# Lower mixture layer: one PE loop of five laps with the last tile's logits inside it, residual and store in halves

## The reference

```python
x = x + xattn(layernorm(x), ctx)        # 32 sequences of 64 rows, 512 wide; keys from ctx (1601 rows)
x = x + attn(layernorm(x))              # causal self-attention, 16 heads
x = x + ffn(layernorm(x))               # the mixture:

def kmoe(x_flat, W_router, A, B, scale, bias, ...):      # 64 experts, top 2
    logits = x_flat @ W_router.T
    vals, idx = jax.lax.top_k(logits, 2)
    probs = softmax(vals)
    xs = x_flat.reshape(-1, d_in1, d_in2)
    Y = einsum('nkoi,nij,nkpj->nkop', A[idx], xs, B[idx])
    return einsum('nkop,nk->nop', Y, probs).reshape(-1, d_out1 * d_out2) * scale + bias

h = gelu(kmoe(x_flat, up...))           # upper layer: rows of 32x32 to 64x64
y = kmoe(h, down...)                    # lower layer: rows of 64x64 back to 32x32
```

## Time and profile before

| | us |
|---|---|
| median of 3 runs | 1514.75 |
| the three runs | 1506.93, 1514.75, 1524.37 |
| the profiled execution, its own time | 1523.18 |
| its span (first to last instruction) | 1521.4 |
| mean granted TensorE clock, share of full | 0.935 |
| PE busy in the span | 1350.5 (89%) |
| DVE busy | 823.1 (54%) |
| ACT busy | 438.3 (29%) |
| POOL busy | 208.2 (14%) |

### The profile page before, as it was taken

One profiled execution on the slowest core, in us unless ns is written; L12 is line 12 of the kernel. 1 busy time (PEld: TensorE's weight loads), 2 busy tenths in 40 slices (PEclk: granted clock), 3 DMA queues, 4 the chain that ended last, 5 costly groups with the idle time before them and its releaser, 6 DMA issues.

```text
span 1521.4 us, 70167 instructions
## 1 busy us (share of the span) xinstructions
PE 1350.5 (89%) x32072; PEld 932.3 (61%) x32072; DVE 823.1 (54%) x1519; ACT 438.3 (29%) x879; POOL 208.2 (14%) x361
## 2 busy tenths in 40 slices
PE   7896799999999999889999999967888988798896
PEld 4895444444544454356666666646777876687785
DVE  1224566666665665145566555633647465347656
ACT  0230121112211221111122222203636455336544
POOL 0000000000000000001111111102424424023212
PEclk9798899999999999999999999968999999959968
DMA  5476187867886789251100111130203012532202
GB/s 194 143 219 217 38 281 273 269 210 278 300 254 213 279 291 285 72 106 56 51 28 31 55 55 42 56 84 30 111 28 139 38 73 105 222 146 87 107 28 83
DMA packets 57228, 211.96 MB, mean 139 GB/s; under 512 B 11760, under 2 KB 28144, under 8 KB 42640
## 3 DMA queue, kind: packets, MB, share of 16 engines
q1 hardware_dynamic: 57104, 210.14, 40.5%
HBM read 172.37 MB, written 37.75 MB: 138 GB/s over the span
## 4 chain that ended last, share of the span: by engine, by line
PE 42%; DVE 6%; issue 5%; ACT 2%; POOL 2%; DMA 1%; SPq 0%; DVEq 0%; POOLq 0%; ACTq 0%
PE ps L895 8%; PE ps L1675 5%; PE ps L1629 4%; PE ps L886 4%; PE ps L996 4%; PE ps L1644 3%; PE ps L1661 2%; PE ps L1718 2%; PE ps L1600 2%; PE ps L916 2%; PE ps L1701 2%; PE ps L1591 1%; PE ps L906 1%; DMA arena<-h_n 1%; PE ps L938 1%
## 5 line engine op out<-in xcount | busy, mean ns | idle before, releaser
L476 DVE STREAM_TRANSPOSE arena<-arena 128x384 f32<-128x384 f32 (+1 forms) x512 | 275.6, 586 | 133.2 <-PE ps L563 132.7
L563 PE MATMUL ps<-arena 32*64 32x224 f32 (+3 forms) x8192 | 241.3, 348 | 30.3 <-issue 22.0
L563 PEld LDWEIGHTS ps<-arena 32*64 32x64 f32 x8192 | 160.6, 134 | 140.9 <-DVE arena L476 85.8
L587 PE MATMUL ps<-arena 128*64 128x512 f32 (+1 forms) x832 | 207.1, 609 | 0.6 <-issue 0.6
L895 PE MATMUL ps<-arena 128*128 128x256 f32 x512 | 116.3, 386 | 6.2 <-ACT arena L847 6.2
L1515 ACT COPY arena<-ps 128x512 f32<-128x512 f32 x128 | 75.1, 587 | 149.8 <-PE ps L1644 79.4
L895 PEld LDWEIGHTS ps<-arena 128*128 128x128 f32 x512 | 97.1, 192 | 21.7 <-ACT arena L847 7.2
L534 ACT ACTIVATE arena<-ps,arena 128x416 f32<-128x416 f32 (+2 forms) x80 | 41.1, 530 | 229.1 <-DVE arena L488 229.1
L587 PEld LDWEIGHTS ps<-arena 128*64 128x64 f32 (+1 forms) x832 | 49.3, 136 | 86.7 <-issue 86.7
L1675 PE MATMUL ps<-arena 64*64 64x32 f32 x4096 | 91.6, 245 | 10.6 <-DVE arena L1352 5.7
L1675 PEld LDWEIGHTS ps<-arena 64*64 64x64 f32 x4096 | 85.8, 164 | 16.0 <-issue 12.5
(11 more groups left out here) (135 smaller groups left out, 1879.0 us busy)
## 6 DMA issues: line engine op xcount, KB each, us to landing
arena<-ctx SPq DMA_DIRECT2D x32, 1792.0 KB
arena<-ctx SPq DMA_DIRECT2D x32, 1280.0 KB
arena<-q_n SPq DMA_DIRECT2D x64, 256.0 KB, 14.0
h_n<-arena SPq DMA_DIRECT2D x16, 1024.0 KB, 4.4
arena<-h_n SPq DMA_DIRECT2D x16, 1024.0 KB, 9.9
arena<-x SPq DMA_DIRECT2D x16, 512.0 KB, 4.6
x_n<-arena SPq DMA_DIRECT2D x16, 512.0 KB, 3.1
arena<-x_n SPq DMA_DIRECT2D x16, 512.0 KB, 3.9
```

The costliest lines, as they stand in the source:

```text
L476: vec.transpose(z[:, at % RING, :, 0:nt * 32].rearrange("p b (j t) -> p b j t", t=32), slots[slot_of(k)][:, :, 0:nt, db * 32:(db + 1) * 32 ...
L563: last = pe.matmul(ps[b * SEQ:(b + 1) * SEQ, tb, g * 224:g * 224 + w], qs[p % 2][r, db, b * SEQ:(b + 1) * SEQ], z[r, at % RING, b, 0:w], s ...
L587: last = pe.matmul(ps[b * SEQ:(b + 1) * SEQ, OB, :], probt[0:r, j, b * SEQ:(b + 1) * SEQ], slot[0:r, b, jj, :], start=j == 0, stop=j == TI ...
```

## The change

The PE loop over tiles becomes a loop over five laps. Lap 0 does the first loop iteration (steps 0 and 1) of tile 0 and then the last tile's logits and their fold. Lap k, from 1 to 4, does the other six iterations of tile k-1, its last two `second_dn`, and the gather of tile k if there is one. The first and last index of the inner loop come out of the lap's number by register arithmetic. PE's wait for the copied logits is gone. On DVE, `parts` and `logits` move from ahead of step 0 to behind `y_out(1)`. `residual` works on halves of 512 columns, behind `y_out` of steps 3, 5, 7 and 9, and SP stores each half by itself; the counts of `s_res` and `s_end` follow.

```diff
             def store_out(T):
                 for t in range(2):
-                    sp.wait_ge(s_res, 2 * T + t + 1)
-                    sp.dma_start(out_v[2 * T + t, :, :], x2b[:, t, :]).then_inc(s_end, 16)
-                sp.wait_ge(s_end, 32 * T + 32)
+                    for half in range(2):
+                        r = slice(half * D, (half + 1) * D)
+                        sp.wait_ge(s_res, 4 * T + 2 * t + half + 1)
+                        sp.dma_start(out_v[2 * T + t, :, r], x2b[:, t, r]).then_inc(s_end, 16)
+                sp.wait_ge(s_end, 64 * T + 64)
...
-            def residual(T, t):
+            def residual(T, t, half):
+                r = slice(half * D, (half + 1) * D)
                 vec.wait_ge(s_x2, 32 * T + 32)
                 vec.wait_ge(s_yt, 2 * T + t + 1)
-                vec.scalar_tensor_tensor(x2b[:, t, :], yt[:, t, :], scales[:, 1:2], x2b[:, t, :],
+                vec.scalar_tensor_tensor(x2b[:, t, r], yt[:, t, r], scales[:, 1:2], x2b[:, t, r],
                                          ALU.mult, ALU.add).then_inc(s_res, 1)
...
-                if T == 0:
-                    parts(T_N, 6)
-                    logits("dn", T_N - 1, 6)
                 for n in range(STEPS):
                     if n + 2 < STEPS:
                         stage_h(T, n + 2)
                     y_out(T, n)
-                    if T and n in (3, 5):
-                        residual(T - 1, n // 5)
+                    if T and n in (3, 5, 7, 9):
+                        residual(T - 1, *divmod((n - 3) // 2, 2))
                     if T == 0:
+                        if n == 1:
+                            parts(T_N, 6)
+                            logits("dn", T_N - 1, 6)
...
-            def steps_dn(T):
-                with pe.Fori(T * 8, T * 8 + 7) as i:
+            def steps_dn(lap):
+                past = [(lap + T_N - k) // T_N for k in range(1, T_N + 1)]
+                whole = past[2] + past[3]
+                with pe.Fori(past[0] + past[1] * 7 + whole * 8, past[0] * 6 + (past[1] + whole) * 8 + 1) as i:
                     second_dn(i * 2, 0)
                     first_dn(i * 2 + 2, 0)
                     second_dn(i * 2 + 1, 1)
                     first_dn(i * 2 + 3, 1)
-                second_dn(T * STEPS + STEPS - 2, 0)
-                second_dn(T * STEPS + STEPS - 1, 1)
...
             gather_dn(0)
-            pe.wait_ge(s_gelu, T_N * STEPS)
-            all_units(pe, 1, 0)
-            logits_dn(6)
-            fold_dn(T_N, 6)
-            pe.wait_ge(s_lge, 9)
-            with pe.Fori(0, T_N) as T:
-                steps_dn(T)
-                with pe.If(T < 1):
-                    transpose_choices("dn", 6, T_N)
-                    for e in range(2):
-                        pe.wait_ge(s_ohe["dn"][e], 4 + CREDIT)
-                with pe.If(T < T_N - 1):
-                    pe.wait_ge(s_oc, T * 2 + 2)
-                    gather_dn(T + 1)
+            with pe.Fori(0, T_N + 1) as lap:
+                steps_dn(lap)
+                with pe.If(lap < 1):
+                    pe.wait_ge(s_gelu, T_N * STEPS)
+                    all_units(pe, 1, 0)
+                    logits_dn(6)
+                    fold_dn(T_N, 6)
+                with pe.If(lap > 0):
+                    second_dn(lap * STEPS - 2, 0)
+                    second_dn(lap * STEPS - 1, 1)
+                    with pe.If(lap < 2):
+                        transpose_choices("dn", 6, T_N)
+                        for e in range(2):
+                            pe.wait_ge(s_ohe["dn"][e], 4 + CREDIT)
+                    with pe.If(lap < T_N):
+                        pe.wait_ge(s_oc, lap * 2)
+                        gather_dn(lap)
```

More of the change, by code:

```diff
@@ L1363, in results_back @@
                 if T:
-                    vec.wait_ge(s_res, 2 * T)
+                    vec.wait_ge(s_res, 4 * T)
                 vec.transpose(yt[:, t, :].rearrange("n (o p) -> n p o", p=D1),
                               y[:, t, :, :].rearrange("q r p -> q p r")).then_inc(s_yt, 1)
-            def residual(T, t):
+            def residual(T, t, half):
+                r = slice(half * D, (half + 1) * D)
                 vec.wait_ge(s_x2, 32 * T + 32)
                 vec.wait_ge(s_yt, 2 * T + t + 1)
-                vec.scalar_tensor_tensor(x2b[:, t, :], yt[:, t, :], scales[:, 1:2], x2b[:, t, :],
+                vec.scalar_tensor_tensor(x2b[:, t, r], yt[:, t, r], scales[:, 1:2], x2b[:, t, r],
                                          ALU.mult, ALU.add).then_inc(s_res, 1)
@@ L1479, in _ @@
             for t in range(2):
-                residual(T_N - 1, t)
+                for half in range(2):
+                    residual(T_N - 1, t, half)
         @block.scalar
```

## The result

The changed kernel takes 1571.16 us (median of 4 runs, 1566.32 to 1581.63), the kernel before in the same job 1516.58 us (4 runs). The ratio is 1.0379, 95% interval 1.0333 to 1.0425. The forecast was 1517 us with a range from 1500 to 1545. Rival 1, *the lap no longer fits*, had said 1537 to 1560, and its mechanism is what happened.

What follows compares the result with a forecast made beforehand. PE's clock, 1.2 or 2.4 GHz, was taken as the largest single thing in the lower layer. Terms +3.2 + 1.0 + 1.1 - 2.5 - 0.5 = +2.3 us on 1514.75 gave 1517 us, range 1500 to 1545.

Steps and rivals of the forecast that it cites:

- Rival 1: PE's longer lap is no longer held, so laps 2 to 4 fetch code again; 1537 to 1560 us, chance 0.22.
- The capacity: PE's loop over laps: the lap's code stays held, so the sum counts no new fetches in laps 2 to 4.
- The price of rival 1: Fetch stops at way back, in steps and at the jump over the logits: 6.8 us a lap, 20 us in all.
- The clock under rival 1: Each fetch stop may drop PE's clock, costing up to 11.4 us on tiles 1 and 3.
- Lap 0: Start of logits to tile 0's second iteration, with steps 0 and 1 first and a 7.0 us jump: +3.2 us.
- Ends of laps and of iterations: PE's loop: two more conditions before step 14's second_dn, +1.0 us; loop limit computed anew each iteration, +1.1 us.
- Residual in halves: DVE's residual: stage_h starts 0.7 us sooner, 0.1 us of wait left at each of four places; -2.5 us.
- Tail: Program's end: the last store starts when the last half is done and carries half as much; -0.5 us.
- rival 3: Lap 0's jump costs 2.67 us or less and tile 0 stays at 2.4 GHz; 1499 to 1500 us, chance 0.12.

Runs made afterwards that it cites:

- pad63: The kernel before plus 63 never-run matmuls behind the last two second_dn inside the loop over tiles; 1517.77 us, ratio 0.9998.
- pad127: The kernel before plus 127 never-run matmuls behind the last two second_dn inside the loop over tiles; 1570.47 us, ratio 1.0329.
- after_short: The changed kernel with half of the last tile's logits left out; 1510.91 us, ratio 0.9963 to the kernel before.
- order_halves: The kernel before with steps 0 and 1 copied ahead of the logits, outside the loop, and residual and store in halves; 1492.68 us, ratio 0.9856.
- halves: The kernel before with only residual and store in halves; 1507.01 us, ratio 0.9934.
- late_loads: The kernel before with SyncE's loads of x2(0) and h(1) held back until TensorE is in the loop's steps; 1517.26 us, ratio 0.9982.
- order_only: The kernel before with steps 0 and 1 of tile 0 in their own code ahead of the logits, residual whole; 1505.20 us, ratio 0.9935.
- nap2: The kernel before with TensorE waiting for two successive small transfers at the lap starts of tiles 1 to 3; 1555.18 us, ratio 1.0269.

## Why the prediction was wrong, step by step

- **The capacity, the step that failed.** The forecast took laps 2 to 4 to fetch nothing. The prediction had counted the change's lap right, 7.4 pieces, eight touched and a ninth asked for ahead, and had named the point, whether eight held pieces are enough. It then gave the failure 0.22, because no row showed a limit. No row showed the opposite either: the longest loop of the trace was 7 pieces. pad63 and pad127 put the limit between eight and nine. That the laps before fetched nothing said only that seven pieces stay, and I let the missing limit count against rival 1 as well.
- **The price of rival 1**, 20 us of stops: measured 25.8. A way back was put at 2.67 us and takes 4.15 to 4.33, and 2.67 us, from a single jump in the upper layer, was too low a row for it; why is not tested. The jump was put at 2.67 us and takes 3.47, 3.63 and, beside the loads of `h`, 6.20. Against these, two stops of 1.2 us in the steps of each lap were counted, and one a lap came, of 0.63 to 1.07 us.
- **The clock under rival 1**, "up to 11.4 us on tiles 1 and 3": measured 12.1 us in tile 1 and 10.2 us in tile 3 after the stops are taken off. Its upper end, 1560, is 20 + 2 x 11.4 us above; of the further 11 us, some 6 are stops and 4 are tile 2, which before had run in part at the high clock.
- *Lap 0*, +3.2 us: with the gather ahead of it, measured 41.91 - 38.95 = +3.0. The stretch of the sum itself, from the gather's end at 1315.00 us to the second iteration, takes 21.24 us against 18.75, +2.5. Code in steps 0 and 1: 1.2 forecast, 1.22 measured. The stop at the jump: 7.0 forecast, 5.46 measured. Logits, `parts` and fold: 9.25 forecast "as before", 10.13 measured (1320.65 to 1330.78), because behind the 1.22 us stop the clock fell for some 3 us: PEclk over them is 0.83, before it was 1.00. So the total is near by two misses that cancel in part.
- *Ends of laps and of iterations*, +1.0 and +1.1 us: in the changed kernel they are covered by the stops, but after_short against order_halves shows them, with the same work on the other engines and PEclk 1.00 in both. Tiles 1 to 3 take 45.23, 45.37 and 35.63 us against 44.74, 44.57 and 34.97, +2.0 us in all. Most gaps at the end of an iteration are 0.43 to 0.46 us against 0.35 to 0.40. Together the two terms were sized about rightly.
- *Residual in halves*, -2.5 us: in `halves` the wait fell from 0.89 to 0.37 us, not to the 0.1 forecast, since a half takes more than half the time. The view of one line of the changed kernel:

```profile
L1374 DVE SCALAR_TENSOR_TENSOR arena<-arena x16: 808/974/976, 1404.8 to 1576.5; 128x512 f32<-128x512 f32 x16
```

  0.97 us against 1.44 for the whole and 0.74 forecast. In the changed kernel the gain was nothing, because its steps in tiles 1 to 3, all at 1.2 GHz, show no wait for DVE.
- *Tail*, -0.5 us: the four last halves take 2.76 us where two whole ones took 2.44, and what follows them, up to the end of the span, 2.52 instead of 3.18. Together -0.3 us.
- **What I thought of tile 0's clock** was wrong too: rival 3 hung it on the 4.71 us stop, and late_loads removed the stop and kept the fall. In order_only and order_halves the clock held through the steps, for a reason that no run isolates. What their traces show is the order: it fell behind the stops in steps 0 and 1 and came back while the logits ran, while in the kernel before it fell at the loop's steps and stayed down until the next gather. Open as well is why tile 2 of before falls in some kernels and not in others after gaps of the same size, and how much of the 10 us of `halves` is that.

## What to carry to other kernels

Count the instructions of every loop body in TensorE's list (a float32 matmul is four), by pieces of 256, the one fetched ahead included, before moving work into the loop. Here eight stayed, and nine cost some 50 us over three laps (pad63, pad127), so work that runs once belongs outside the body, even at the price of a second copy of some steps. A stop of TensorE can cost more than its length (31.4 us of span for 8.7 us of stops in nap2): price it with the low clock of the stretch behind it, from the trace's own rows at either clock.

## What the runs showed of the hardware

- PE keeps eight pieces of 256 instructions with the one fetched ahead (pad63, no packet behind 1385 us), not nine (pad127, 24 packets). Beyond the limit all pieces of the lap are fetched anew, 9 a lap, not the one too many.
- A piece asked for ahead came after 3.4 us with the queues nearly empty (late_loads) and after 7.0 us beside the loads of `x2` and `h`.
- Three stops of 3.9 us without a fetch cost 37 us in the median (1555.18 against 1518.17), of which 8.7 are the stops.
- A residual of 128x512 took VectorE 0.97 us in the steps where 128x1024 took 1.44; at the program's end, 0.69 (2.76/4) against 1.22 (2.44/2).
